# Second layer of a two-layer transformer: order of the constant loads, and the shape of the transfers into its attention

## The reference

```python
x = x + _L0_attn_ref(xn, ...) + _L0_ffn_ref(xn, ...)          # layer 0
xn = _layernorm(x, axis=-1)
x = x + _L1_attn_ref(xn, ...) + _L1_ffn_ref(xn, ...)          # layer 1

# _L1_attn_ref, s = 1024 tokens, NH = 32, NKV = 8, HD = 64
q = (hidden_states @ q_w.T).reshape(b, s, NH, HD).transpose(0, 2, 1, 3)
k_r = hidden_states @ kr_w.T                   # the rotated half of each key
...
q = q * cos + _rotate_half(q) * sin
k = k * cos + _rotate_half(k) * sin
c_kv = hidden_states @ down_w.T
k_c = c_kv @ upk_w.T                           # the half that is not rotated
v = (c_kv @ upv_w.T).reshape(b, s, NKV, HD).transpose(0, 2, 1, 3)
...
scores = jnp.einsum('bhqd,bhkd->bhqk', q, kf) / sqrt(HD)      # causal mask
out = jnp.einsum('bhqk,bhkd->bhqd', softmax(scores), v)
return out.transpose(0, 2, 1, 3).reshape(b, s, NH * HD) @ o_w.T
```

## Time and profile before

| | |
|---|---|
| median of 3 runs | 2372.4 us (2368.79 to 2374.82) |
| profiled execution: its own time | 2372.37 us |
| its span, first to last instruction | 2370.6 us |
| granted TensorE clock, mean over the span | 0.966 |
| busy in the span: PE, DVE, ACT, POOL | 89%, 65%, 37%, 20% |
| DMA queue of SP | 187648 packets, 239.59 MB, 32.5% of 16 engines |

### The profile page before, as it was taken

The page is one execution under the profiler, slowest core; times in us unless marked ns, Lnnn a source line. Parts: engine busy times, 40 slices in busy tenths (PEclk is TensorE's granted clock), DMA queues, the critical chain, the costliest instruction groups (busy, mean ns, idle before and its releaser), DMA issues. The chain is left out here.

```text
span 2370.6 us, 54461 instructions
## 1 busy us (share of the span) xinstructions
PE 2121.0 (89%) x22256; PEld 1479.6 (62%) x22256; DVE 1544.9 (65%) x2534; ACT 874.1 (37%) x1836; POOL 480.0 (20%) x408
## 2 busy tenths in 40 slices
PE   5899969999996999958898888888888699999997
PEld 4577747777775878834444444444444588787776
DVE  4544333488884544448988899988899440377776
ACT  3322113222222310025655555655656321234443
POOL 0110111212120135510111111111111344212111
PEclk9999989999998999978999999999999899999999
DMA  4221135133325543333333343333443455320100
GB/s 156 73 84 43 53 113 202 38 111 100 109 75 196 170 150 124 112 104 77 91 98 85 87 113 100 91 100 82 101 112 82 153 196 186 124 98 19 54 1 36
DMA packets 188737, 243.00 MB, mean 103 GB/s; under 512 B 38272, under 2 KB 111296, under 8 KB 185824
## 3 DMA queue, kind: packets, MB, share of 16 engines
q1 hardware_dynamic: 187648, 239.59, 32.5%
q10 hardware_dynamic: 864, 0.21, 0.0%
HBM read 156.82 MB, written 82.90 MB: 101 GB/s over the span
## 5 line engine op out<-in xcount | busy, mean ns | idle before, releaser
L1591 ACT ACTIVATE a_prob<-ps,a_nmax 128x256 f32<-128x256 f32 (+7 forms) x512 | 377.6, 740 | 353.7 <-DVE a_nmax L1619 214.0
L1704 PE MATMUL ps<-a_kt,a_q 64*128 64x512 f32 (+5 forms) x1536 | 382.8, 540 | 86.6 <-ACT a_prob L1591 63.3
L1619 DVE TENSOR_REDUCE a_nmax<-ps 128x1 f32<-128x1024 f32 (+3 forms) x256 | 257.3, 1005 | 75.7 <-PE ps L1704 74.0
L1636 DVE STREAM_TRANSPOSE a_pt_long<-a_prob 128x512 f32<-128x512 f32 (+3 forms) x512 | 279.2, 586 | 0.0
L1704 PEld LDWEIGHTS ps<-a_kt,a_q 64*128 64x128 f32 x1536 | 144.1, 194 | 186.0 <-ACT a_prob L1591 115.9
L1718 PE MATMUL ps<-a_pt_long,a_v 32*64 32x256 f32 (+3 forms) x7808 | 229.7, 346 | 1.6 <-DVE a_pt_long L1636 0.2
L1998 DVE SCALAR_TENSOR_TENSOR f_part<-ps,f_gu_scale,f_part 128x512 f32<-128x512 f32 x264 | 184.8, 746 | 65.5 <-PE ps L2045 52.2
L1718 PEld LDWEIGHTS ps<-a_pt_long,a_v 32*64 32x64 f32 x7808 | 154.3, 132 | 105.1 <-issue 76.7
L1671 POOL TENSOR_TENSOR a_o<-a_left 128x256 f32<-128x256 f32 x128 | 90.5, 729 | 597.3 <-ACT a_left L1601 597.3
L907 POOL TENSOR_TENSOR f_hT_lo<-f_h,f_hT_hi 128x512 fp32r<-128x512 f32 x64 | 82.6, 1303 | 324.5 <-ACT f_hT_hi L890 324.5
L1701 PE MATMUL ps<-a_causal,a_identb 64*128 64x128 bf16 x1024 | 112.9, 225 | 39.2 <-ACT a_prob L1591 39.2
(11 more groups left out here) (228 smaller groups left out, 4599.0 us busy)
## 6 DMA issues: line engine op xcount, KB each, us to landing
a_q<-scratch_QT SPq DMA_DIRECT2D x512, 64.0 KB, 2.1
scratch_QT<-k_qo SPq DMA_DIRECT2D x64, 256.0 KB, 2.3
a_v<-scratch_V SPq DMA_DIRECT2D x64, 256.0 KB, 4.7
scratch_OT<-a_o SPq DMA_DIRECT2D x32, 512.0 KB, 3.3
o_of<-scratch_OT SPq DMA_DIRECT2D x32, 512.0 KB, 4.1
f_block<-in_packed SPq DMA_DIRECT2D x33, 256.0 KB, 3.4
a_kt<-scratch_KT SPq DMA_DIRECT2D x128, 64.0 KB, 4.0
f_xt_hi<-scratch_xt SPq DMA_DIRECT2D x6, 1024.0 KB, 7.7
```

Of the source, the lines that this page charges most:

```text
L1591: last = nc.scalar.activation(prob[:, n % PRING, s].rearrange("p (a w) -> p a w", w=w), SC[n % 2][:, a, 0:w], ACT.Exp, bias=nmax[:, n % 4, ...
L1619: nc.vector.tensor_reduce(nmax[:, n % 4, 0:1], SC[n % 2][:, :, 0:width(0, t)], AX.XY, ALU.max, negate=True).then_inc(maxed, 1)
L1636: last = nc.vector.transpose(pt[hf][:, lo:hi, h, t - FIRST[hf], :], src.rearrange("p (j k) -> p j k", k=32))
L1704: last = pe.matmul(sc[:, a, 0:w], q[r, slot, heads[a * hf], :], kt[r, b, keys], start=not masked, stop=True, skip_group_check=True)
```

## The change

In `projections1` SP's first loads come in a new order: `eps` and `ident` with a semaphore of their own (`first_in`), then the four weights, then the four tables, with `c_in` for these alone. ACT and PE wait at their start for `first_in`; DVE waits for the tables after its first split of the transposed x, no longer ahead of it.

The scratch tensor `QT` is laid out anew: for each of 32 coordinates p the 4 heads h follow each other, where before the heads came first. The store of a half chunk therefore names its rows on the DRAM side as 4 x 32, and is still one transfer of 128 rows. The halves j of the coordinates now follow each other evenly, so one transfer brings 64 coordinates. The keys come with one transfer for each copy, and V with one transfer in all, which reads the same source four times. The counts that PE waits for follow.

One more edit is outside: in `attention0` the semaphore `tables` is gone, and `prepared`, which had reached 4, takes its place with the count 5.

```diff
-                                        ).then_inc(tables, 1)
-                dve.wait_ge(tables, 1)
+                                        ).then_inc(prepared, 1)
+                dve.wait_ge(prepared, 5)
...
-        CONSTS = [(ident[:], d["c_ident"]), (eps[:], d["c_eps"]), (cosk[:], d["c_cosk"]), (sink[:], d["c_sink"]),
-                  (cosq[:], d["c_cosq"]), (sinq[:], d["c_sinq"])]
+        CONSTS = [(cosk[:], d["c_cosk"]), (sink[:], d["c_sink"]), (cosq[:], d["c_cosq"]), (sinq[:], d["c_sinq"])]
...
-                for n, name in enumerate(names[:2]):
+                sp.dma_start(eps[:], d["c_eps"]).then_inc(first_in.sem, 16)
+                sp.dma_start(ident[:], d["c_ident"]).then_inc(first_in.sem, 16)
+                for n, name in enumerate(names):
                     sp.dma_start(staged(n), d[name].rearrange("(k p) n -> p k n", p=P)).then_inc(w_in[n].sem, 16)
                 for dst, src in CONSTS:
                     sp.dma_start(dst, src).then_inc(c_in.sem, 16)
-                for n, name in enumerate(names[2:], 2):
-                    sp.dma_start(staged(n), d[name].rearrange("(k p) n -> p k n", p=P)).then_inc(w_in[n].sem, 16)
...
-                        sp.dma_start(d["QT"][bass.ds(g, 1), i, :, c * CH:(c + 1) * CH].squeeze(0), qo[:, c % 2, i, :]
+                        sp.dma_start(d["QT"][bass.ds(g, 1), i, :, :, c * CH:(c + 1) * CH].squeeze(0).rearrange("p h t -> h p t"),
+                                     qo[:, c % 2, i, :]
                                      ).then_inc(q_stored[c % 2].sem, 16)
...
-                act.wait_ge(c_in.sem, ALL_CONSTS)
+                act.wait_ge(first_in.sem, 32)
...
+                split_turned(0)
                 dve.wait_ge(c_in.sem, ALL_CONSTS)
-                split_turned(0)
...
-                pe.wait_ge(c_in.sem, ALL_CONSTS)
+                pe.wait_ge(first_in.sem, 32)
...
                     for a in range(2):
-                        for j in range(2):
-                            r = a * HD1 + j * HD1 // 2
-                            sp.dma_start(q[r:r + HD1 // 2, k % QRING, :, :],
-                                         d["QT"][g, j, :, tok].rearrange("(h p) t -> p h t", h=HQ)
-                                         ).then_inc(q_in[k % QRING], 16)
+                        sp.dma_start(q[a * HD1:(a + 1) * HD1, k % QRING, :, :],
+                                     d["QT"][g].rearrange("j p h t -> (j p) h t")[:, :, tok]
+                                     ).then_inc(q_in[k % QRING], 16)
...
+                    src = d["KT"][:, g * 16:(g + 1) * 16, b * SEQ:(b + 1) * SEQ]
                     for a in range(2):
-                        for part in range(4):
-                            r = a * HD1 + part * 16
-                            sp.dma_start(kt[r:r + 16, b, :],
-                                         d["KT"][part, g * 16:(g + 1) * 16, b * SEQ:(b + 1) * SEQ]
-                                         ).then_inc(kt_in, 16)
+                        sp.dma_start(kt[a * HD1:(a + 1) * HD1, b, :], src).then_inc(kt_in, 16)
...
-                    for i in range(4):
-                        sp.dma_start(v[32 * i:32 * i + 32, b, :, :], d["V"][g, b, :, :, :]).then_inc(v_in, 16)
+                    sp.dma_start(v[:, b, :, :], d["V"][g, b, :, :, :].unsqueeze(0).broadcast_to([4, 32, SEQ // 32, HD1])
+                                 ).then_inc(v_in, 16)
...
-                        pe.wait_ge(kt_in, 16 * 8 * (unit + 1))
+                        pe.wait_ge(kt_in, 16 * 2 * (unit + 1))
-                        pe.wait_ge(q_in[slot], 64 * (k // QRING + 1))
+                        pe.wait_ge(q_in[slot], 32 * (k // QRING + 1))
-                            pe.wait_ge(v_in, 64 * (unit + 1))
+                            pe.wait_ge(v_in, 16 * (unit + 1))
...
-    d["QT"] = scratch("QT", [NKV, 2, P, T])
+    d["QT"] = scratch("QT", [NKV, 2, HD1 // 2, 4, T])
```

More of the change, by code:

```diff
@@ L158, in attention0 @@
         w_hi, w_lo, prepared = sem("w_hi"), sem("w_lo"), sem("prepared")
-        tables_exp, tables = sem("tables_exp"), sem("tables")
+        tables_exp = sem("tables_exp")
         ln, ln_std = sem("ln"), sem("ln_std")
@@ L1081, in projections1 @@
         apart = sig("apart", 0)
-        c_in = sig("c_in", 0)
+        first_in, c_in = sig("first_in", 0), sig("c_in", 0)
         w_in = [sig(f"w_in{i}", 0) for i in range(len(weights))]
```

## The result

The changed kernel takes 2490.4 us (median of 6 runs, 2484.4 to 2499.1) against 2369.3 us for the kernel before in the same session (2366.0 to 2374.8): a ratio of 1.0509, 95% interval 1.0486 to 1.0533. It is 121 us slower; the forecast was 260 us slower, with a range from +3 to +363. The numbers read from a profile are those of one execution of each kernel. The direction and the range held, the size did not.

A forecast was written before the change was run, and what follows sets the result against it. Loads bound only the starts of `projections1` and `attention1`; between them PE, then the loop of DVE and ACT, set the pace. From 2372.4 us, -7.5 + 129 + 0 + 138 = +259.5 gave 2632 us, range 2375 to 2735.

The forecast's parts named there:

- Four engines: Query stores, key loads and V, outermost count 4, run on 4 of 16 engines; chance 0.55 with crowding, 0.25 without.
- The first rival: All transfers still run on 16 engines, only the gains come: -12.9 us, 2359.5 us; chance 0.17.
- Start of `projections1`: `eps` and `ident` load first, so ACT's square root starts when its table load ends: -7.5 us, between 5 and 9.5 gained.
- The stores: Query stretch: 64 stores on four engines that crowd, three quarters of the way between +22 and +165: +129 us.
- the uncrowded bound of +22: Query stretch, four engines at 22.7 GB/s each: stores 185 us, with query weights 195 us in place of 172.9.
- the V row: Profile row of V's loads to 32 partitions at a time, 213 GB/s: 12.8 GB/s per engine, taken as the crowded rate.
- Start of `attention1`: Fewer issues up to `a_ones` save 5.4 us, but keys on four engines delay the landing, 13.7 against 13.8 us: 0.
- The bound of -3: Start of `attention1` if the four engines don't crowd: -3 us.
- The units: `attention1`: PE waits for query tiles behind V and keys on four engines, 8.8 us for 16 units: +138 us.
- Tile 4's 2.8 us: `attention1` units: query tile 4, behind V and the keys (9.0 us), lands 30.6 us after V's issue, 2.8 late.
- the clock: `attention1` units: clock may fall in PE's waits, up to 3 us a unit, another 48 at most; put at 0.
- The second rival: Four engines but no crowding: -7.5 + 22 - 3 = +11.5 us, 2384 us; chance 0.25.

The follow-up runs named there:

- the last two runs: Kernel before with first part, 128-row even stores, V in four transfers, `attention1` first loads reordered; keys in two transfers: 2363.9 us, in eight: 2359.0 us.
- the other edit: Changed kernel with V's transfer in parts of 28 rows, to partitions 0, 28, 56, 84, plus a transfer of the 16 rows left: 2390.3 us.

## Why the prediction was half right

- **Four engines.** Right, and the root of the result. The Trainium skill's rule ("DMA: Bandwidth & Descriptors", section "Why a DMA increments its semaphore by 16 and not by 1") gives four engines for these transfers, and the packets agree: four at once for V and the stores named as 4 x 32 rows, 16 for V as an even run of 128. The first rival (2359.5) falls.
- **Start of `projections1`.** -7.5 forecast, -7.3 measured, in the changed kernel and alone.
- **The stores: the step that failed.** +129 was forecast, three quarters of the way from the time at 22.7 GB/s for each engine to that at 12.8; the way was not gone at all (21.0), and the stretch grew by 15.5 us, a little under the uncrowded bound of +22. That four busy engines would set the pace of the stretch was right; the rate at which they go was the part that was wrong. The mechanism, pairs of engines 32 partitions apart that crowd, is borne out by V, but the V row, from which the 12.8 was taken, has rows of 8 KB with 16 engines on 32 partitions, and the stores have rows of 2 KB with four engines on 128. The prediction carried the figure from one to the other, and so 113 us of its 260 never came.
- **Start of `attention1`.** 0 forecast, 0.04 measured. It had been reckoned from the keys' landing on four engines (13.7 us), and the last two runs, which differ in the keys' transfers alone, show that keys on four engines hold the start back (15.1 us against 10.2). The bound of -3 for engines that don't crowd should be -3.8 by the prediction's own terms (0.9 + 0.7 + 1.6 + 5.3 + 1.5 = 10.0 against 13.8); that changes nothing else.
- **The units.** +138 forecast, +112 measured. Tile 3 was to be 6.0 us late and was 6.5. Tile 4's 2.8 us did not come: the keys ahead of it had been reckoned with 9.0 us. At the 5.3 us that the prediction has for engines that don't crowd, tile 4 would land 26.9 us after V's issue, before its use at 27.8; and the keys' packets of 4 KB do take 159 ns at the median in the changed kernel's units, 25.8 GB/s. In its place came the clock, put at 0: 7.5 us a unit less 6.5 of wait leaves about 1 for products at the lower clock, by subtraction. That the forecast's 8.8 us a unit came near the 7.5 is in part luck, since the term that didn't come was made up in part by one that had been put at nothing.
- **The second rival** (four engines, no crowding, 2384) was right for the stores and wrong for V. The truth lay between it and the forecast, with each right at one place: -7.3 + 15.5 + 112 = 120.

Still open: how much of the 12 us that remain in the kernels with parts of 28 rows comes from the extra transfer of 16 rows; and why V's place in DRAM is worth 22 us by itself and nothing beside the other edit. Why long rows crowd and short ones don't isn't shown either; that engines with short rows drift apart sooner would fit, but no run looked at it.

## What to carry to other kernels

Before transfers are merged, or a scratch layout is regrouped, look at the outermost count that is left on each side: 128 rows named as 4 x 32 ran on 4 of 16 engines, and one such transfer of 1 MB in front of a small urgent load cost 112 us over 15 uses, while four transfers, or the same one behind the urgent load, cost nothing. Fewer issues gained nothing measurable here: in the units no engine waited for a load, and at the start of `attention1`, where PE does wait for the last one, the 4.8 us saved in issues were lost again behind keys on four engines. When a rate is borrowed from another row of the profile for a cost estimate, it must have the same row length and the same number of engines on the same partitions.

## What was not expected of the hardware

- The crowding of engines that write 32 partitions apart depends on the rows: 15.8 GB/s for each busy engine with 8 KB, 19.6 with 2 KB, 21.3 with 8 KB when the parts don't meet.
- A store named as 4 x 32 rows took 544 ns to issue on SP for 332 as 128 rows. Long transfers on few engines also hold up the issues behind them: query tiles 4 and 5, four issues, took 16.27 us in the changed kernel, and 2.54 with V in four.
- A wait of 6.6 us for PE once a unit was enough for the granted clock to fall from 1.00 (2.4 GHz) to 0.50 (1.2 GHz) in the 6.5 us from the end of the wait, a mean of 0.59 over the 14 us that hold both; PE's product then took 0.90 us for 0.50.
- Parts that follow each other evenly in DRAM are joined: the packets of four neighbouring units in one transfer were under way for 3.5 us in one unit, up to 16 and more at once, and those of the four equal ones for 17.7, four at once.
